# Unread matmuls at batch starts, an earlier base for the last block, and the first expert requested alone

## The chip, the cores and the metric

One core of one Trainium2 chip runs the whole program. The metric is the device time of one execution in microseconds (us). A difference is judged against the spread of repeated executions of both kernels on the same chip.

## What is computed

`x` has 12,500 rows of 256, and 212,500 directed edges (with one self loop a row) are sorted by target. Cut to what matters:

```python
xn = _layernorm(x)
agg = segment_sum(xn[src], dst) / counts                       # mean over the neighbours
gnn = relu(agg @ W_l.T + b_l + xn @ W_r.T) + xn
q, k, v = elu(xn@wq+bq)+1, elu(xn@wk+bk)+1, xn@wv+bv            # 8 heads of 32
mix = ((q @ (k.T @ v)) / (q @ k.sum(0))) @ wo + bo             # linear attention
x1 = x + gnn + mix
y = _layernorm(x1)
logits = mean(y, rows) @ Wr + br                               # one routing decision for all rows
p = softmax(logits); p = softmax(p * scale); w, e = top_k(p, 2); w = softmax(w)
h = sum_i w_i * (gelu(y @ W1[e_i] + b1[e_i]) @ W2[e_i] + b2[e_i])
out = x1 + _layernorm(h + y) * gamma + beta
```

## The kernel before, in words

Stage 1 (up to about 142 us) normalises the rows, writes them to DRAM as a table of two f16 parts (`xn_table`), and turns the edge lists.

Stage 3 (142 to 2760 us) sums the neighbours. The rows are cut into 49 blocks of 256 targets. A block has 34 tiles of 128 edges (29 in the last block). For each tile POOL gathers 128 rows of the table into its slot of the ring (L672), DVE makes a one-hot matrix (L1504), and PE multiplies the two in two f16 matmuls (L1243, L1244, "the rows"), adding into one of two PSUM banks of `pa`. The tiles come in 8 batches a block, which begin at k = 0, 4, 8, 13, 17, 21, 25 and 30. POOL may be eight batches ahead: it gathers batch q of the next block once `batch_used` says that PE has used batch q of this one, and once `idx_ready` says that ACT has written its indices (L738). ACT takes a strip of 64 finished sums (L768) four times a block; strips begin at k=4, 13, 21 and 30. DVE joins the strips (L1513 to L1522) and ACT scales them (L775).

Between the rows PE does other work, at tiles written out by hand:
- blocks 0 to 9 ("shadow"): the keys of the attention (`key_work`, L982, L995, L1005);
- blocks 10 to 19 ("doubled"): the dense work of two blocks in each (`double_work`), with `normalizers` at k=12, 13 and k=29, 30;
- blocks 20 to 48 ("late", a loop from about 1295 us on): the dense work of one block (`dense`). At k=1, 2 stands `mixed_product` of the block before (L1094), at k=9 `turn_sums` (L1145, waits for L775), at k=12, 13 `neighbour_product` (L1094), at k=14 `turn_xn` (L1070, taken by ACT L781), at k=16, 17 `queries` (L1078), which ACT reads in L790 (exponent) and L793, at k=24, 25 `normalizers` (L1087, waits for DVE's L1548; DVE goes on with L1554, a reciprocal L1556 and L1558), at k=27 `turn_y` (L1134, taken by ACT L815), and at k=29, 31 `base` (L1105, L1094, L1108, L1109), after which ACT makes the next rows (L762) and SP asks for the x rows after them (L296).

ACT's queue in a late block is L768, L790, L793, L807, L738 for two batches, L768, L815, L738 for three batches, L768, L762, L738, L768, L775, L738, L768, L800, L781. Each instruction waits in its queue behind those before it.

Behind the last rows of the last block PE does both halves of `base`, then the rest of that block's dense work. A mean over all y gives the logits (L1258). DVE finds the two best experts in small steps (L1669 to L1702) and writes both indices with one copy (L1696, `picked`). SP waits for it, reads both registers (L613), and asks for W1, b1 and W2 of each expert (L615, L617, L620), and then b2 (L624). ACT and DVE split each W1 into two parts (L950, L1719).

Stage 5 (about 2813 us to the end) runs both experts on 512 rows at a time: L1275 (first layer), L1290 (second).

## Time and profile before

| | us |
|---|---|
| runs | 3372.62, 3365.61, 3381.5 |
| median | 3372.62 |
| the profiled execution, its time | 3382.15 |
| its span | 3380.7 |
| stage 1 | 0 to 142 |
| shadow blocks | 142 to 695 |
| doubled blocks | 695 to 1295 |
| late blocks | 1295 to 2760 |
| last block's rest, routing | 2760 to 2813 |
| experts | 2813 to 3380 |

A time in a row is counted in us from the start of the span. PE is TensorE's matrix product, DVE VectorE, ACT ScalarE, POOL GpSimd, SP the engine that issues most transfers. A row of an engine in time gives the start, the length, the line, the tiles written and read, how many instructions it stands for, and in brackets the idle time before it and what ended that. "remote" and "issue" are releases for which the profile has no name.
### The profile page before, as it was taken

What the parts mean: (1) busy time and instruction counts of PE and PEld (TensorE: products, weight loads), DVE (VectorE), ACT (ScalarE), POOL (GpSimd) and SP (SyncE); (2) the same over time, 40 slices, a digit from 0 to 9 for tenths busy, and PEclk for the clock granted to TensorE, in tenths of its full rate; (3) what the DMA queues carried; (4) which work ended last, traced back from release to release, by engine and by line L of the source; (5) the groups of instructions that cost most, each with busy time, mean ns of one, the idle gap of its engine ahead of it and who ended that gap; (6) DMA issues with size and microseconds to landing.
All of it is one profiled execution on the core that took longest, in us unless ns stands there. A gap on an engine that the chain in (4) does not pass through costs nothing.

```text
span 3380.7 us, 35327 instructions
## 1 busy us (share of the span) xinstructions
PE 2141.0 (63%) x10858; PEld 1625.9 (48%) x10858; DVE 1423.6 (42%) x3244; ACT 955.7 (28%) x2221; POOL 1607.6 (48%) x1679
## 2 busy tenths in 40 slices
PE   1147667657766775565465454654555557999998
PEld 0135445545444553343343333433333346999997
DVE  7612222334444443332333323333333335777777
ACT  4512222222222221111111111111111114656565
POOL 1256666665555555666566665666566640000000
PEclk9978788878777777767767777677777778999999
DMA  6633333333333333333333333333333322222221
GB/s 210 215 101 115 112 111 110 91 102 106 100 97 100 98 93 103 98 103 98 98 101 100 103 101 96 100 101 102 98 98 103 103 70 77 75 63 68 74 74 58
DMA packets 205191, 340.31 MB, mean 101 GB/s; under 512 B 33118, under 2 KB 151131, under 8 KB 205115
## 3 DMA queue, kind: packets, MB, share of 16 engines
q0 software_dynamic: 80160, 219.14, 22.6%
q1 hardware_dynamic: 124538, 119.81, 11.1%
q8 instruction: 42, 0.69, 0.1%
q10 hardware_dynamic: 416, 0.39, 0.1%
q14 instruction: 35, 0.28, 0.0%
HBM read 288.01 MB, written 51.20 MB: 100 GB/s over the span
## 4 chain that ended last, share of the span: by engine, by line
PE 41%; another core or an unknown queue 34%; issue 9%; ACT 7%; DVE 7%; DMA 1%; ACTq 1%; SPq 0%; DVEq 0%
PE pd L1290 8%; PE pd L1094 6%; PE pa L1275 4%; PE pc L1275 4%; PE pa L1244 3%; PE pd L995 2%; PE pa L1243 2%; PE pd L1105 2%; PE pd L1087 2%; PE pd L1134 1%; PE pc L1005 1%; PE pc L1145 1%; PE pd L1108 1%; PE pd L1109 1%
## 5 line engine op out<-in xcount | busy, mean ns | idle before, releaser
L672 POOL DMA_INDIRECT ring<-xn_table,idxb x1661 | 1598.8, 963 | 1150.4 <-issue 633.2
L1244 PE MATMUL pa<-ring,ohh 128*128 128x257 f16 x1661 | 472.0, 305 | 76.4 <-issue 76.2
L1243 PE MATMUL pa<-ring,ohh 128*128 128x256 f16 x1661 | 469.9, 304 | 75.0 <-issue 65.9
L1087 PE MATMUL pd<-work,KS_s 128*128 128x256 f32 x196 | 107.8, 652 | 472.3 <-DVE work L1548 395.5
L1290 PE MATMUL pd<-parts 128*128 128x256 f32 (+1 forms) x1568 | 312.2, 282 | 1.8 <-DVE parts L1747 1.8
L1087 PEld LDWEIGHTS pd<-work,KS_s 128*128 128x128 f32 x196 | 49.7, 313 | 489.0 <-DVE work L1548 404.6
L1244 PEld LDWEIGHTS pa<-ring,ohh 128*128 128x128 f16 x1661 | 179.8, 108 | 197.0 <-issue 121.8
L1094 PE MATMUL pd<-mats,work 128*128 128x256 f32 x784 | 260.1, 463 | 0.9 <-DVE work L1530 0.9
L1290 PEld LDWEIGHTS pd<-parts 128*128 128x128 f32 (+1 forms) x1568 | 253.1, 188 | 10.3 <-DVE parts L1747 2.4
L1504 DVE TENSOR_TENSOR ohh<-pc,edges 128x512 f16<-128x512 f32 (+1 forms) x307 | 214.2, 718 | 98.4 <-PE pa L1244 64.6
L768 ACT ACTIVATE ring<-pa 128x257 f32<-128x257 f32 x196 | 75.4, 385 | 620.1 <-remote 313.5
L1243 PEld LDWEIGHTS pa<-ring,ohh 128*128 128x128 f16 x1661 | 180.8, 109 | 129.3 <-issue 86.7
L1513 DVE TENSOR_TENSOR ring<-ring 64x514 f32<-64x514 f32 x49 | 33.5, 684 | 445.0 <-ACT ring L768 445.0
L1290 PE MATMUL pd<-W_lo_t,parts 128*128 128x256 f32 x784 | 219.7, 280 | 0.0
L1094 PEld LDWEIGHTS pd<-mats,work 128*128 128x128 f32 x784 | 164.2, 232 | 114.2 <-issue 91.7
L1548 DVE SCALAR_TENSOR_TENSOR work<-work 128x512 f32<-128x512 f32 x49 | 33.9, 692 | 425.3 <-ACT work L793 413.7
L790 ACT ACTIVATE work<-pd,bq_c 128x256 f32<-128x256 f32 x98 | 41.1, 471 | 535.0 <-remote 523.4
L995 PE MATMUL pd<-mats,yT 128*128 128x256 f32 x392 | 124.2, 472 | 103.0 <-ACT yT L723 102.5
L1145 PE MATMUL pc<-ident,ring 128*128 128x128 f32 x160 | 39.9, 397 | 209.1 <-ACT ring L775 209.1
L1556 DVE RECIPROCAL work<-work 128x512 f32<-128x512 f32 x49 | 164.3, 3353 | 1.7
L995 PEld LDWEIGHTS pd<-mats,yT 128*128 128x128 f32 x392 | 90.2, 242 | 128.9 <-ACT yT L723 112.8
L1290 PEld LDWEIGHTS pd<-W_lo_t,parts 128*128 128x128 f32 x784 | 147.2, 188 | 9.1
(205 smaller groups left out, 3726.1 us busy)
## 6 DMA issues: line engine op xcount, KB each, us to landing
ring<-xn_table,idxb POOLq DMA_INDIRECT x1661
yT<-in_x SPq DMA_DIRECT2D x48, 512.0 KB
xn_table<-ring SPq DMA_DIRECT2D x24, 512.0 KB, 5.4
x_rows<-work SPq DMA_DIRECT2D x48, 256.0 KB
y_rows<-work SPq DMA_DIRECT2D x48, 256.0 KB
work<-y_rows SPq DMA_DIRECT2D x24, 512.0 KB, 4.3
work<-x_rows SPq DMA_DIRECT2D x24, 512.0 KB, 3.7
out<-work SPq DMA_DIRECT2D x24, 512.0 KB, 3.1
```

The lines of the kernel that those rows point to most:

```text
L672: pool.indirect_dma_start(out=msgs[:, k, 0:PARTS * D], out_offset=None, in_=xn_table[:, :], in_offset=bass.IndirectOffsetOnAxis(ap=idxb[:, ...
L768: nc.scalar.activation(strips[:, (NS * u + t + 1) % KEPT, 0:D + 1], pa[:, t % 2, 0:D + 1], ACT.Copy)\
L995: ins = mm(pd[0:n, 2 + pr, (t % 2) * D:(t % 2 + 1) * D], xTb[kq % 2][:, c, t * P:t * P + n], wk_s[:, c, :], start=c == 0, stop=c == C - 1)
L1087: ins = mm(pd[:, 0, c * BN:(c + 1) * BN], KS_s[:, c, :], pq[:, c * BN:(c + 1) * BN], start=True, stop=True)
L1094: ins = mm(pd[:, 2 + h, at:at + D], a[:, c * BN + h * P:c * BN + (h + 1) * P], w[:, c, :], start=False, stop=last and c == C - 1, skip_gro ...
L1145: ins = nc.tensor.transpose(to[:, c * BN + g * P:c * BN + (g + 1) * P], strips[:, NS * u + 2 * g + 1, c * P:(c + 1) * P], ident[:, :])
L1243: mm(pa[:, t % 2, 0:D], oh[:, slot, :], msgs[:, k, 0:D], start=begins, stop=False, skip_group_check=True)
L1244: ins = mm(pa[:, t % 2, 0:D + 1], oh[:, slot, :], msgs[:, k, D:2 * D + 1], start=False, stop=ends, skip_group_check=True)
L1275: ins = mm(hbank(f)[:, 0:w], wp[:, e, c, fc * P:(fc + 1) * P], yp[u][:, c, 0:w], start=c == 0 and wp is W1_hi and yp is y_hi, stop=c == C ...
L1290: ins = mm(pd[0:n, 2 * u + t // 2, (t % 2) * D:(t % 2 + 1) * D], hp[:, t * P:t * P + n], wp[:, f, :], start=f == 0 and t % 2 == 0 and hp i ...
L1504: V.tensor_tensor(oh[:, slot:slot + m, :], bc(row[:, c0:c0 + WIN], m), where, ALU.is_equal)\
L1556: V.reciprocal(qb, qb).then_inc(s["nrm_rec"], 1)
```

## The change

Three edits.

(a) `occupy(b, q, bank)` issues a number of unread matmuls at the first tile of each batch, ahead of that tile's dense work and ahead of its waits for one-hots and gathers. Each is an f32 matmul of the identity against 252 columns of `blo_b` into columns 260 to 511 of the bank of `pa` that the tile uses; the sums use columns 0 to 256, and nobody reads the others. Late blocks get `FILL`, doubled blocks `FILL_DOUBLE`, shadow blocks one of two `FILL_KEYS`. The wait for `strip_taken` moves ahead of the fills and the dense work.

(b) In the last block both normalizers and the first half of `base` are issued at k=21 and the second half at k=25, in place of the normalizers at k=24 and 25 and of both halves behind the last rows.

(c) DVE writes the first expert's index as soon as it is known and raises `picked`; SP then reads that register alone and asks for this expert's W1 in two halves, b1 and W2, and only then waits for the second. ACT and DVE split W1 in three pieces, and the first layer's first two column groups wait for the first piece only.

```diff
+        W1_PIECES = [(0, "w1_loaded0", 16, slice(0, F // 2)), (0, "w1_half1", 32, slice(F // 2, F)),
+                     (1, "w1_loaded1", 32, slice(0, F))]
...
-            sp.wait_ge(s["picked"], 1)
-            chosen = [sp.value_load(pick[0:1, n:n + 1], min_val=0, max_val=NE - 1) for n in range(2)]
-            for n, e in enumerate(chosen):
-                sp.dma_start(W1_s[:, n, :, :], W1[bass.ds(e, 1), :, :].rearrange("a (c p) f -> p (a c) f", p=P))\
-                    .then_inc(s[f"w1_loaded{n}"], 16)
+            chosen = []
+            for n in range(2):
+                sp.wait_ge(s["picked"], n + 1)
+                e = sp.value_load(pick[0:1, n:n + 1], min_val=0, max_val=NE - 1)
+                chosen.append(e)
+                if n == 0:
+                    sp.dma_start(W1_s[:, n, :, 0:F // 2], expert_rows(e, 0, F // 2)).then_inc(s["w1_loaded0"], 16)
+                    sp.dma_start(W1_s[:, n, :, F // 2:F], expert_rows(e, F // 2, F)).then_inc(s["w1_half1"], 16)
+                else:
+                    sp.dma_start(W1_s[:, n, :, :], expert_rows(e, 0, F)).then_inc(s["w1_loaded1"], 16)
...
-            for e in range(2):
-                act.wait_ge(s[f"w1_loaded{e}"], 32)
-                nc.scalar.activation(W1_hi[:, e, :, :], W1_s[:, e, :, :], ACT.Copy).then_inc(s["w1_hi_made"], 1)
+            for e, loaded, count, fs in W1_PIECES:
+                act.wait_ge(s[loaded], count)
+                nc.scalar.activation(W1_hi[:, e, :, fs], W1_s[:, e, :, fs], ACT.Copy).then_inc(s["w1_hi_made"], 1)
...
+            FILL_KEYS = ((0, 3, 0, 0, 0, 0, 0, 1), (4, 3, 0, 1, 4, 3, 0, 5))
+            FILL_DOUBLE = (0, 0, 0, 6, 0, 0, 0, 3)
+            FILL = (0, 3, 7, 1, 0, 7, 5, 0)
+            UNREAD = slice(D + 4, 512)
+
+            def occupy(b, q, bank):
+
+                if isinstance(b, int) and b < 2 * DELAY:
+                    n = (FILL_KEYS[b % 2] if b < DELAY else FILL_DOUBLE)[q]
+                else:
+                    n = FILL[q]
+                for _ in range(n):
+                    mm(pa[:, bank, UNREAD], ident[:, :], blo_b[:, 0:512 - (D + 4)], start=False, stop=False,
+                       skip_group_check=True)
...
+            LAST_BASE = (21, 25)
...
-                if k in DENSE:
+                if is_int(b, NB - 1) and k in LAST_BASE:
+                    if k == LAST_BASE[0]:
+                        for c in range(C):
+                            normalizers(b, c)
+                    base(b, LAST_BASE.index(k), u)
+                elif k in DENSE and not (is_int(b, NB - 1) and k > LAST_BASE[0]):
...
                     for k in ks:
+                        slot = k % SLOTS
+                        t = LO[k] // STRIP
+                        begins = is_int(b, 0) and k == 0 or k > 0 and LO[k] != LO[k - 1]
+                        ends = last_block and k == LAST - 1 or k + 1 < TB and LO[k] != LO[k + 1]
+                        if begins:
+                            wait(pe, s["strip_taken"], NS * b + t)
+                        if k == ks[0]:
+                            occupy(b, q, t % 2)
                         if isinstance(b, int) and b < DELAY:
                             key_work(b, k, u)
...
-                if last_block:
-                    for h in range(2):
-                        base(b, h, u)
...
-                    pe.wait_ge(s["w1_split"], e + 1)
+                    pe.wait_ge(s["w1_split"], 1 if f < FC // 2 else e + 2)
...
             first_at(row(R_W), row(R_M, 1), 0)
+            V.tensor_copy(pick[:, 0:1], row(R_I, 1)).then_inc(s["picked"], 1)
...
-            V.tensor_copy(pick[:, :], row(R_I, 2)).then_inc(s["picked"], 1)
+            V.tensor_copy(pick[:, 1:2], row(R_I, 1, 1)).then_inc(s["picked"], 1)
...
-            split_w1(0)
+            split_w1(0)
+            split_w1(1)
```

## Rows read from the trace of the kernel before

**Rows 1.** The page: busy time, share of the span and instructions; shares of the last chain.

```profile
PE 2141.0 (63%) x10858; PEld 1625.9 (48%) x10858; DVE 1423.6 (42%) x3244; ACT 955.7 (28%) x2221; POOL 1607.6 (48%) x1679
...
PE 41%; another core or an unknown queue 34%; issue 9%; ACT 7%; DVE 7%; DMA 1%; ACTq 1%; SPq 0%; DVEq 0%
```

**Rows 2.** By stretch, core 0: length, busy (instructions) of each engine, TensorE clock, DMA.

```profile
1300.00:2650.00 1350.00, 726.29 (x3323) 500.02 (x3323) 443.41 (x931) 225.71 (x723) 837.47 (x876) 0.73 0.34 100
...
2813.00:3380.00 567.00, 555.12 (x3552) 502.56 (x3552) 399.90 (x902) 329.15 (x524) 0.00 (x0) 0.99 0.22 70
...
1795.94:1848.54 52.60, 27.13 (x130) 18.50 (x128) 17.15 (x36) 8.77 (x28) 32.59 (x35) 0.76 0.34 100
803.30:861.80 58.50, 39.54 (x186) 27.84 (x184) 26.17 (x58) 15.22 (x45) 32.36 (x34) 0.85 0.35 104
```

**Rows 3.** POOL in time, late block: start, us, instruction [idle before <-releaser].

```profile
1795.94 0.94 POOL L672 DMA_INDIRECT ring<-xn_table,idxb  x1 [6.34 <-ACT idxb L738]
...
1820.81 1.33 POOL L672 DMA_INDIRECT ring<-xn_table,idxb  x1 [3.91 <-issue]
...
1848.54 0.95 POOL L672 DMA_INDIRECT ring<-xn_table,idxb  x1 [6.35 <-ACT idxb L738]
```

**Rows 4.** The page's costliest groups: busy, mean ns, idle before, its releaser.

```profile
L672 POOL DMA_INDIRECT ring<-xn_table,idxb x1661 | 1598.8, 963 | 1150.4 <-issue 633.2
...
L790 ACT ACTIVATE work<-pd,bq_c 128x256 f32<-128x256 f32 x98 | 41.1, 471 | 535.0 <-remote 523.4
```

**Rows 5.** ACT in time, the same late block.

```profile
1792.42 0.84 ACT L790 ACTIVATE work<-pd,bq_c 128x256 f32<-128x256 f32 x2 [14.67 <-remote]
...
1799.88 0.39 ACT L738 ACTIVATE idxb<-edges 128x4 int32 x3
...
1818.04 1.09 ACT L762 ACTIVATE work<-work,nmr_a,rstd_a 128x256 f32<-128x256 f32 x2 [13.19 <-remote]
```

**Rows 6.** PE in time, the same late block.

```profile
1778.99 1.03 PE L1078 MATMUL pd<-work,mats 128*128 128x256 f32 x4
...
1794.77 1.22 PE L1087 MATMUL pd<-work,KS_s 128*128 128x256 f32 x2 [13.18 <-DVE work L1548]
...
1801.69 0.59 PE L1108 MATMUL pd<-ring,ident 128*128 128x256 f32 x2
1802.12 0.59 PE L1109 MATMUL pd<-work,ident 128*128 128x256 f32 x2
...
1823.58 1.11 PE L1145 MATMUL pc<-ident,ring 128*128 128x128 f32 x4 [3.98 <-ACT ring L775]
```

**Rows 7.** PE and ACT in time, another late block.

```profile
2260.55 1.91 PE L1078 MATMUL pd<-work,mats 128*128 128x256 f32 x4
...
2264.78 0.84 ACT L790 ACTIVATE work<-pd,bq_c 128x256 f32<-128x256 f32 x2 [6.58 <-remote]
```

**Rows 8.** By stretch of 2 us, the late block of rows 3.

```profile
1796.00:1798.00 2.00, 2.00 (x9) 1.43 (x8) 0.69 (x1) 0.00 (x0) 1.69 (x2) 0.50 0.51 162
1800.00:1802.00 2.00, 2.00 (x8) 1.15 (x7) 1.97 (x2) 0.27 (x3) 1.58 (x2) 1.00 0.45 131
1822.00:1824.00 2.00, 0.42 (x2) 0.42 (x3) 1.13 (x4) 1.00 (x3) 1.39 (x3) 0.50 0.22 66
```

**Rows 9.** PE in time, a doubled block at the lower clock.

```profile
827.21 1.06 PE L1108 MATMUL pd<-work,ident 128*128 128x256 f32 x2
```

**Rows 10.** POOL in time, a doubled block.

```profile
853.32 0.94 POOL L672 DMA_INDIRECT ring<-xn_table,idxb  x1 [4.26 <-PE pa L1244]
```

**Rows 11.** PE in time, the end of stage 3 and the routing.

```profile
2779.27 1.12 PE L1105 MATMUL pd<-blo_b,ones 1*128 1x512 f32 x2
...
2785.13 1.89 PE L1094 MATMUL pd<-M_s,work 128*128 128x256 f32 x8
...
2812.96 1.19 PE L1275 MATMUL pa<-parts 128*128 128x512 f32 x2 [6.90 <-DVE W_lo_t L1719]
```

**Rows 12.** SP's queue in time: the first request of an expert's weights.

```profile
2806.03 0.41 SPq L615 DMA_DIRECT2D mats<-in_L_ffn_W  x1
```

More of the change, by code:

```diff
@@ L252, in build_layer @@
         names = """waits_taken iota_set iota_float iota_placed mask_step wk_loaded consts_set ident_set raw_padded raw_loaded raw_float raw_turned raw_taken
-            flag_sum flag_added flag_set w_loaded biases_loaded wlr_turned wlr_taken bias1_set
+            flag_sum flag_added flag_set w_loaded biases_loaded wlr_turned wlr_taken
             x_loaded0 x_loaded1 x_loaded2 x_loaded3 p1_bn p1_mv p1_rstd p1_stats rows_unscaled hi_made lo_made xn_ready xn_stored0 xn_stored1 xn_stored2 xn_stored3 xt_turned xt_made
@@ L261, in build_layer @@
             route_step route_exp logits_made ysum_made mean_made picked gates_made gates_spread gates_taken
-            w1_loaded0 w1_loaded1 w2_loaded0 w2_loaded1 b2_loaded w1_hi_made w1_split w2_hi_made w2_split yh_made yl_made hh_made hl_made
+            w1_loaded0 w1_half1 w1_loaded1 w2_loaded0 w2_loaded1 b2_loaded w1_hi_made w1_split w2_hi_made w2_split yh_made yl_made hh_made hl_made
             l2_done b2_made yin_loaded0 yin_loaded1 yb_made xb_made
@@ L609, in _, with expert_rows @@
             over_blocks(sp, transfers)
-            sp.wait_ge(s["picked"], 1)
-            chosen = [sp.value_load(pick[0:1, n:n + 1], min_val=0, max_val=NE - 1) for n in range(2)]
-            for n, e in enumerate(chosen):
-                sp.dma_start(W1_s[:, n, :, :], W1[bass.ds(e, 1), :, :].rearrange("a (c p) f -> p (a c) f", p=P))\
-                    .then_inc(s[f"w1_loaded{n}"], 16)
+            def expert_rows(e, f0, f1):
+                return W1[bass.ds(e, 1), :, f0:f1].rearrange("a (c p) f -> p (a c) f", p=P)
+            chosen = []
[8 more added lines that the diff above has]
+                    sp.dma_start(W1_s[:, n, :, :], expert_rows(e, 0, F)).then_inc(s["w1_loaded1"], 16)
                 sp.dma_start(b1_c[:, n, :], b1[bass.ds(e, 1), :].rearrange("a (c p) -> p (a c)", p=P),
                              allow_slow_non_contiguous=True)\
-                    .then_inc(s[f"w1_loaded{n}"], 16)
+                    .then_inc(s["w1_half1" if n == 0 else "w1_loaded1"], 16)
                 sp.dma_start(W2_s[:, n * FC:(n + 1) * FC, :],
@@ L1234, in stage3 @@
                             pe.wait_ge(s[f"gathered{q}"], batch_gathers(b, q))
-                        slot = k % SLOTS
-                        t = LO[k] // STRIP
-                        begins = is_int(b, 0) and k == 0 or k > 0 and LO[k] != LO[k - 1]
-                        ends = last_block and k == LAST - 1 or k + 1 < TB and LO[k] != LO[k + 1]
-                        if begins:
-                            wait(pe, s["strip_taken"], NS * b + t)
                         if is_int(b, 0) and k == 0:
@@ L1465, in _ @@
             dve.wait_ge(s["wk_loaded"], 32)
-            V.tensor_scalar(b1k_b[:, :], b1k_b[:, :], 1.0, None, ALU.add).then_inc(s["bias1_set"], 1)
-            dve.wait_ge(s["bias1_set"], 1)
+            V.tensor_scalar(b1k_b[:, :], b1k_b[:, :], 1.0, None, ALU.add).then_inc(s["mask_step"], 1)
+            dve.wait_ge(s["mask_step"], 4)
             dve.wait_ge(s["p1_stats"], len(TABLE_GROUPS))
@@ L1714, in _, with split_w1 @@
             split_y(0, 0)
-            def split_w1(e):
-                dve.wait_ge(s["w1_hi_made"], e + 1)
-                V.tensor_tensor(W1_lo[:, e, :, :], W1_s[:, e, :, :], W1_hi[:, e, :, :], ALU.subtract)\
+            def split_w1(piece):
+                e, _, _, fs = W1_PIECES[piece]
+                dve.wait_ge(s["w1_hi_made"], piece + 1)
+                V.tensor_tensor(W1_lo[:, e, :, fs], W1_s[:, e, :, fs], W1_hi[:, e, :, fs], ALU.subtract)\
                     .then_inc(s["w1_split"], 1)
@@ L1735, in mix_b2 @@
                 V.tensor_scalar(b2a, b2_b[:, 0, :], gate_b[:, 0:1], None, ALU.mult).then_inc(s["mask_step"], 1)
-                dve.wait_ge(s["mask_step"], 4)
+                dve.wait_ge(s["mask_step"], 5)
                 V.scalar_tensor_tensor(out=b2m, in0=b2_b[:, 1, :], scalar=gate_b[:, 1:2], in1=b2a, op0=ALU.mult,
@@ L1803, in stage5 @@
                     if is_int(q, 0) and f < 3:
-                        (lambda: split_w1(1), lambda: split_w2(1), mix_b2)[f]()
+                        (lambda: split_w1(2), lambda: split_w2(1), mix_b2)[f]()
                     if f == 0 and later:
```

## The prediction

> **What bounds the kernel now.** I read the busy shares first, then the chain that ended last, then the costliest groups. No engine is full: TensorE is busy 63% of the span and POOL 48%, and the chain gives 41% to PE and 34% to releases that the profile can't name [rows 1]. So the answer differs by stage, and the table by stretch shows it [rows 2]. From 2813 us on (the two experts) PE is busy 555 of 567 us at a clock of 0.99: full, and no wait there to fill. From 1300 to 2650 us PE is busy 726 of 1350 us at a mean clock of 0.73, and POOL 837. There POOL's gathers set the pace: a run of 17 lasts from 1795.94 to 1820.81 - 3.91 = 1816.90, one every 1.25 us, so the 34 of a block need 42.5 us, and a block takes 52.6 (1795.94 to 1848.54) [rows 3]. The ten missing microseconds are two gaps a block: 6.34 us ahead of batch 3, waiting for ACT's indices L738, and 3.91 us ahead of batch 7. Gaps of that kind are all that a change in this stage can return: L672's idle time is 1150.4 us [rows 4]; less 1,660 usual pauses of 0.30 us it is 650, the wait for the table at the start still in it. That is the outer bound.
>
> What ends those gaps? ACT's exponent L790 stands idle 523.4 us for a release "remote" [rows 4]. In the block shown it starts at 1792.42, and by PE's records the queries L1078 that it reads had begun their second half at 1778.99 [rows 5, 6]. It starts 2.8 us after the last gather of the run has ended (1795.94 - 6.34 = 1789.60). L762 starts at 1818.04 although L1109 was recorded by 1806, 1.1 us after that run ended. So while POOL gathers, late PE results reach the others only when the run is over: the two gaps are partly a closed loop, run, release, indices, next run. One block speaks for the loop's stiffness: L1078's second half is recorded at 2260.55 there, hardly two microseconds before the end of its run, L790 starts at 2264.78 [rows 7], and the gap behind it is of the usual size. PE's queries may come 10 us late, or early, and the period is the same.
>
> The Trainium skill ("Perfetto Trace Analysis", "Tensor Engine Instruction (MATMUL, LD_WEIGHTS)") says that a matmul's recorded end is estimated, and that its semaphore goes out only after PSUM has acknowledged the writes. By that PE's gap in front of L1087 need not be free time, and fills put there could queue behind unfinished work; the trace neither shows nor excludes it.
>
> **The clock.** PE stalls 13.18 us ahead of L1087 and 3.98 us ahead of L1145 [rows 6]. In both the granted clock falls to its lower level (0.50, 1.2 GHz) and is still there when PE resumes: 0.50 in 1822 to 1824 and in 1796 to 1798, 1.00 in 1800 to 1802 [rows 8]. So some 5 us of work behind L1087 (1794.77 to the 1800 of that row) and, by the same table cut finer, 3 us behind L1145 run at half speed: 2.5 and 1.5 us that a full clock would give back.
>
> **Part (a), the unread matmuls.** A fill is one f32 matmul of the identity against 252 columns. Its nearest rows are L1108 and L1109, the identity against 256 columns: two records each, starting 0.43 us apart at the full clock [rows 6]. At half each record is 1.06 us long in place of 0.59 [rows 9], and I take 0.85 us a fill. Late blocks get 0+3+7+1+0+7+5+0 = 23, so 9.9 us at the full, 19.6 us at the half clock, and the 29 of them 287 to 567 us of PE time. Doubled blocks get 9 (90 in all), shadow blocks 4 or 20 (120): another 90 to 180 us. None of it costs anything where PE waits anyway, and PE is idle 25.5 us a late block (52.6 less 27.1 [rows 2]).
> - k=4 (3) and k=8 (7) stand ahead of L1145, which waits for the chain of strip, join and scaling. PE has 4 us there [rows 6]; ten fills take 4.3 us warm, 8.5 us cold. So they overhang by 0 to 4.5 us, and give back the 1.5 us of a cold resumption.
> - k=21 (7) stand ahead of L1087's 13 us stall: 3 us, hidden. But they run at its beginning, so 10 us of idle time stay behind them and PE resumes cold as before: the 2.5 us there are not won.
> - k=25 (5) stand between the two halves of L1087, right after the resumption, at the half clock: 4.3 us (2.1 warm) that nothing hides. Behind them wait L1554, the reciprocal, L1134, L815 and ACT's L738 x3 at 1799.88, the indices of batches 5, 6 and 0 [rows 5]. POOL needs the first of them for the ninth gather of its run, 1795.94 + 8 x 1.25 = 1805.9. L738 would come at 1802 to 1804.2: in time, with 1.7 us to spare in the worse case.
> - k=13 (1): 0.4 us.
> The strip_taken wait moved ahead of the fills holds back only neighbour_product's second half at k=13, behind a strip taken 5 us before: nothing.
>
> What reaches POOL? Behind L1145 up to 1.5 us a block, if the earlier queries shorten the gap ahead of batch 3; nothing, if the loop holds. I take 0.9 us, nearer to the upper end than a mean of the two, because some releases do come through in the first eight microseconds of a run: 28 x 0.9 = **-25 us** (bounds: -42 from the clock, +126 from 4.5 us of overhang).
>
> In the doubled blocks PE is busy 39.5 of 58.5 us at a mean clock of 0.85 [rows 2], and POOL waits for PE's rows (4.26 us at 853.32 [rows 10]). A mean of 0.85 between two levels, 0.5 and 1, means 30% of the time at half. But the nine fills (3.8 us warm, 7.7 cold) stand at k=13 (6) and k=30 (3), each time between the halves of a normalizer, right behind its stall. They warm the clock by delaying L1134 and the rows behind. The row that POOL waits for (k=12) is ahead of them, and the five gathers that it then starts (6.3 us) cover 5.1 us of fills. Gain and loss nearly cancel: **-5** (bounds -4.26 x 10 = -43, that wait gone in each block, to +7.7 x 10 = +77). Shadow blocks: PE mostly waits for rows and keys; 12 fills a block on the mean; **-5** (-50 to +50).
>
> The Trainium skill ("TensorE: Matmul & The Clock Gate", "Loop structure matters more than you think") has a loop that waits for a transfer between its matmuls drop to the slow clock, as here. It asks for dense real work, not for filler; by its reading alone, all 4 us a block would come back, and the sum would be 3382 - 112 before the rest.
>
> **Part (b), the last block.** Both normalizers and base(0) move to k=21, base(1) to k=25. They are the same instructions. Before, base ran behind the last rows from 2779.27 to 2785.13, and L1145, which waits for the last strip's join, came 1.7 us later, behind eight L1094 [rows 11]. Moved ahead, the 5.9 us are off that place; but the last rows then end up to 5.9 us plus five fills later, and join and scaling (5 us from the strip to L1145) start behind them. PE waits for little in this stretch, so I expect little: **+1** (-3 to +6).
>
> **Part (c), the first expert.** The first index is copied before the second is searched, some eight DVE steps of about 0.18 us, 1.5 us, earlier; SP reads one register instead of two, and the first W1 request, at 2806.03 [rows 12], carries half. The two steps that split it, ACT's and DVE's, halve too: L1275, at 2812.96 after 6.90 us of waiting [rows 11], could start 2.5 us sooner. The second half and its queue come at the old time or 0.5 us later. **-2.5** (-4 to +1).
>
> **Sum.** -25 - 5 - 5 + 1 - 2.5 = -36.5. The profiled execution has a span of 3380.7 and a time of 3382.15 us, 9.5 above the median of the runs. 3382.15 - 36.5 = 3345.7; less 9.5: **3336 us**, 1.1% faster. Chance 0.36.
>
> **Rivals.**
> 1. The loop holds and hides everything: fills in idle time, earlier queries released at the run's end as before. For it: the block of [rows 7], and the two gaps ahead of batch 3, 6.34 and 6.35 us [rows 3]. Left are the tail and a few us in the doubled blocks: 3365 us. Chance 0.26. That the fills don't warm the clock at all belongs here.
> 2. Slower: the fills push a release out of the part of a run in which it still comes through. The place is k=8 and k=25: if L1145, through L1070 and L781, or L1134 passes that point, the indices of batch 5 come only after POOL has stopped once more, and each stop costs what the gap ahead of batch 7 costs, 3.91 us [rows 3]. In 28 blocks that is +109: 3482 us; in a third of them, or by the overhang alone (1 to 2 us a block), 3400 to 3430. It decides when L738 x3 comes more than 6 us later than now, or L1145 more than 3. Chance 0.30.
> 3. The queries get ahead of the point: batch 3's indices are there before batch 2 is gathered, and the 6.34 us go in every late block. 28 x 6.34 = 178, so 3195 us. PE would have to be 3 us earlier and has 1.5. Chance 0.08.
>
> **How the numbers follow.** About 0.5% (17 us) is what a measurement of this kernel can tell from no change. Faster holds the forecast (0.36) and rival 3 (0.08): 0.44. Same 0.26. Slower 0.30. The range leaves out rival 3 and the full case of rival 2, some 0.15 to 0.2 together: 3240 to 3465. As cases of both signs are likely, the forecast's own range is 3280 to 3356.
>
> **What would show it.** POOL's period of 52.6 us in the late loop is the first thing to read: 51.7 if I am right, 52.6 for rival 1, 56 for rival 2, 46 for rival 3. The clock should be 1.00 when L1145 resumes and 0.50 when L1087 does. L738 x3 should come 2 to 4 us later against the run's start, and the run of 17 gathers stay whole. In the tail, L1275 should start earlier against L1258, and L1145 about as late behind the last gather. I am wrong if the clock at L1145's resumption is still 0.50, or if the runs of gathers have other lengths than 17.

## The result and the profile after

| | us |
|---|---|
| before, median of 4 runs | 3373.14 (3365.61 to 3381.5) |
| changed, median of 4 runs | 3440.96 (3430.06 to 3470.29) |
| ratio, with its 95% interval | 1.0227 (1.0193 to 1.0262) |
| changed, profiled execution | 3451.18, span 3449.7 |

The change costs 2.3%. Lines of `kernel.py` have moved: L672 is now L683, L738 L749, L781 L792, L790 L801, L1070 L1081, L1078 L1089, L1087 L1098, L1134 L1145, L1145 L1156, L1244 L1278, L1275 L1306, L768 L779, L775 L786, L1094 L1105, L1105 L1116, L1504 L1535, L1513 L1544, L1516 L1547, L1548 L1579, L1558 L1589, L1719 L1752; the fills are L1172.

The changed kernel's page, the parts of [rows 1] and [rows 4]:

```profile
PE 2442.2 (71%) x12612; PEld 1916.6 (56%) x12612; DVE 1424.2 (41%) x3246; ACT 952.4 (28%) x2222; POOL 1605.7 (47%) x1679
...
PE 42%; another core or an unknown queue 29%; issue 14%; DVE 7%; ACT 6%; DMA 1%; ACTq 0%; SPq 0%; POOL 0%; DVEq 0%; POOLq 0%
...
L683 POOL DMA_INDIRECT ring<-xn_table,idxb x1661 | 1596.9, 961 | 1217.3 <-issue 548.8
L1172 PE MATMUL pa<-blo_b,ident 128*128 128x252 f32 x1754 | 475.9, 416 | 35.0 <-issue 33.5
```

PE is busy 301 us more than before: the 877 fills take 475.9 us, and the other work, at a higher clock, some 175 us less. In the chain the share of unnamed releases falls from 34% to 29% and that of "issue" rises from 9% to 14%. Yet POOL's idle time grows by 67 us, from 1150.4 to 1217.3, and the span by 69: nearly the whole loss is gathers that start later. By stretch, and by two pieces of one late block, with the columns of [rows 2]:

```profile
1300.00:2650.00 1350.00, 896.03 (x4250) 661.05 (x4250) 421.17 (x887) 212.95 (x691) 793.77 (x830) 0.82 0.32 95
...
2297.89:2355.18 57.29, 35.72 (x174) 26.98 (x173) 17.33 (x36) 8.58 (x28) 32.58 (x35) 0.79 0.31 92
2320.00:2322.00 2.00, 2.00 (x11) 1.80 (x10) 0.00 (x0) 0.00 (x0) 1.68 (x2) 1.00 0.43 127
2347.00:2349.00 2.00, 1.59 (x4) 1.32 (x5) 0.00 (x0) 0.36 (x1) 0.00 (x0) 0.50 0.00 0
```

The clock did rise: 0.82 in the late loop against 0.73. The gain that it was to bring isn't there. One late block takes 57.29 us, of which 15.0 us are its two gaps (11.95 and 3.02) and 42.3 its gathers with their usual pauses. POOL in time, as in [rows 3]:

```profile
2297.89 0.94 POOL L683 DMA_INDIRECT ring<-xn_table,idxb  x1 [12.08 <-ACT idxb L749]
...
2315.60 0.95 POOL L683 DMA_INDIRECT ring<-xn_table,idxb  x1 [3.02 <-remote]
...
2355.18 0.94 POOL L683 DMA_INDIRECT ring<-xn_table,idxb  x1 [11.95 <-ACT idxb L749]
```

The gaps are now ahead of batch 3 (11.95 or 12.08 us, before 6.34) and ahead of batch 6 (3.02 us at 2315.60, before none), and the one ahead of batch 7 is gone. Runs are of 12 and 22 gathers instead of 17 and 17. Not every late block is like this one: of the runs that start in blocks 20 to 47, 23 are of 12 gathers, 9 of 22, 20 still of 17 and 19 of other, mostly shorter, lengths (before, 52 of 58 are of 17). Summed over these blocks, the gaps ahead of batch 6 grow by 47 us and those ahead of batch 7 shrink by 59, so the new stop replaces the old one and by itself adds nothing. The gaps ahead of batch 3 grow by 67 us (from 177 to 244), those ahead of batches 1 and 2 by 20. PE and ACT in the same block, as in [rows 6] and [rows 5]:

```profile
2295.45 3.14 PE L1172 MATMUL pa<-blo_b,ident 128*128 128x252 f32 x14
...
2299.10 0.59 PE L1098 MATMUL pd<-work,KS_s 128*128 128x256 f32 x2
...
2299.75 2.29 PE L1172 MATMUL pa<-blo_b,ident 128*128 128x252 f32 x10
2301.87 0.59 PE L1098 MATMUL pd<-work,KS_s 128*128 128x256 f32 x2
...
2319.50 3.14 PE L1172 MATMUL pa<-blo_b,ident 128*128 128x252 f32 x14
...
2322.70 0.60 PE L1156 MATMUL pc<-ident,ring 128*128 128x128 f32 x4
...
2326.88 0.60 PE L1081 MATMUL pd<-ident,work 128*128 128x128 f32 x4
...
2347.41 2.07 PE L1089 MATMUL pd<-work,mats 128*128 128x256 f32 x4 [19.49 <-ACT work L792]
```

```profile
2304.25 0.39 ACT L749 ACTIVATE idxb<-edges 128x4 int32 x3
...
2318.65 0.91 ACT L786 ACTIVATE ring<-ring,cnts 128x256 f32<-128x256 f32 x2 [1.95 <-DVE cnts L1553]
...
2346.76 0.60 ACT L792 ACTIVATE work<-pd 128x512 f32<-128x512 f32 x1 [12.71 <-remote]
2351.66 0.84 ACT L801 ACTIVATE work<-pd,bq_c 128x256 f32<-128x256 f32 x2 [4.30 <-PE pd L1089]
```

Read the last two PE rows with the last two ACT rows. PE turned the rows (L1081) at 2326.88; ACT copied them (L792) only at 2346.76, 3.5 us behind the end of a run of gathers (2355.18 - 11.95 = 2343.23). PE waited 19.5 us for that copy, did the queries at the lower clock (0.50 in 2347 to 2349), and L801 came at 2351.66. The same steps in the kernel before, POOL, PE and ACT, in the run that ends ahead of the first gather of [rows 3]:

```profile
1768.22 1.32 POOL L672 DMA_INDIRECT ring<-xn_table,idxb  x1 [3.77 <-issue]
...
1776.52 0.60 PE L1070 MATMUL pd<-ident,work 128*128 128x128 f32 x4
...
1777.15 0.60 ACT L781 ACTIVATE work<-pd 128x512 f32<-128x512 f32 x1
```

There the copy L781 starts as soon as the rows are turned, 8.3 us into the run, and only L790 is withheld. In the change one more step of the chain stands behind the end of the run: L792, queries and L801 take 4.9 us plus 0.84, and the gap has grown by 5.6.

This holds beyond the one block. In the traces of the nine kernels that met this condition (the two here, and e1 to e4 and e16 to e18 below) I took blocks 21 to 47, 243 blocks in all. In 47 of them the copy starts behind the last gather of the run, and the gap ahead of batch 3 is 8.6 to 12.2 us. In the other 196 it starts earlier, and the gap is never over 7.8 us. The kernel before has no block of the first kind, the change 17 of 27. The rows are turned 8.1 us into their run of gathers in the kernel before and 9.8 us in the change (medians).

By the starts of the gathers the loss splits so (us, changed against before): blocks 0 to 19, 1090.6 against 1097.2; blocks 20 to 47, 1546.7 against 1478.1; block 48, 43.8 against 40.7; from the last gather's start to the end, 626.5 against 622.5. The others nearly cancel (-6.6 + 3.1 + 4.0 = +0.5); the late blocks hold 68.6 of 69.1 us.

### The profile page after: what moved, and what is told of

It reads as the page before. It is cut to its first block, busy times and chain, and to the rows that moved or that the text cites. A ratio compares the mean times of both kernels' runs of the same rounds, so it can differ in the third digit from the quotient of the medians.

```text
span 3449.7 us, 38842 instructions
## 1 busy us (share of the span) xinstructions
PE 2442.2 (71%) x12612; PEld 1916.6 (56%) x12612; DVE 1424.2 (41%) x3246; ACT 952.4 (28%) x2222; POOL 1605.7 (47%) x1679
## 4 chain that ended last, share of the span: by engine, by line
PE 42%; another core or an unknown queue 29%; issue 14%; DVE 7%; ACT 6%; DMA 1%; ACTq 0%; SPq 0%; POOL 0%; DVEq 0%; POOLq 0%
PE pd L1321 8%; PE pa L1172 5%; PE pd L1105 4%; PE pc L1306 4%; PE pa L1306 4%; PE pc L1016 3%; PE pd L1089 3%; PE pd L1006 2%; PE pa L1278 2%; PE pa L1277 2%; PE pd L1116 2%; PE pd L1098 1%; DVE bst L1369 1%; ACT ring L779 1%
## 5 line engine op out<-in xcount | busy, mean ns | idle before, releaser
L683 POOL DMA_INDIRECT ring<-xn_table,idxb x1661 | 1596.9, 961 | 1217.3 <-issue 548.8
L1172 PE MATMUL pa<-blo_b,ident 128*128 128x252 f32 x1754 | 475.9, 416 | 35.0 <-issue 33.5
L1277 PE MATMUL pa<-ring,ohh 128*128 128x256 f16 x1661 | 440.2, 287 | 49.7 <-issue 39.5
L1278 PE MATMUL pa<-ring,ohh 128*128 128x257 f16 x1661 | 441.2, 288 | 37.1 <-issue 36.5
L1172 PEld LDWEIGHTS pa<-blo_b,ident 128*128 128x128 f32 x1754 | 358.3, 215 | 98.8 <-issue 51.8
L1089 PE MATMUL pd<-work,mats 128*128 128x256 f32 x392 | 147.8, 515 | 344.5 <-ACT work L792 285.1
L1089 PEld LDWEIGHTS pd<-work,mats 128*128 128x128 f32 x392 | 91.8, 259 | 371.6 <-ACT work L792 296.5
L779 ACT ACTIVATE ring<-pa 128x257 f32<-128x257 f32 x196 | 74.8, 382 | 785.8 <-remote 537.9
L1535 DVE TENSOR_TENSOR ohh<-pc,edges 128x512 f16<-128x512 f32 (+1 forms) x307 | 214.8, 718 | 186.1 <-remote 138.0
L1278 PEld LDWEIGHTS pa<-ring,ohh 128*128 128x128 f16 x1661 | 170.0, 102 | 163.8 <-issue 83.6
L1105 PE MATMUL pd<-mats,work 128*128 128x256 f32 x784 | 225.6, 412 | 42.7 <-DVE work L1561 28.5
L1105 PEld LDWEIGHTS pd<-mats,work 128*128 128x128 f32 x784 | 142.9, 199 | 141.5 <-issue 92.5
L1016 PE MATMUL pc<-yT 128*128 128x257 f32 x392 | 125.2, 475 | 84.5 <-DVE yT L1417 47.6
L1579 DVE SCALAR_TENSOR_TENSOR work<-work 128x512 f32<-128x512 f32 x49 | 34.0, 693 | 329.7 <-ACT work L804 254.7
L1098 PE MATMUL pd<-work,KS_s 128*128 128x256 f32 x196 | 71.6, 452 | 137.8 <-DVE work L1579 111.4
L1568 DVE TENSOR_TENSOR work<-work,pd 128x512 f32<-128x512 f32 x49 | 33.7, 687 | 316.7 <-ACT work L811 175.1
```

Source lines behind the costliest of these rows:

```text
L683: pool.indirect_dma_start(out=msgs[:, k, 0:PARTS * D], out_offset=None, in_=xn_table[:, :], in_offset=bass.IndirectOffsetOnAxis(ap=idxb[:, ...
L779: nc.scalar.activation(strips[:, (NS * u + t + 1) % KEPT, 0:D + 1], pa[:, t % 2, 0:D + 1], ACT.Copy)\
L1016: ins = mm(pc[:, c, 0:KXW], phi[0:n, t, c * P:(c + 1) * P], xnb[kq % 2][0:n, t, :], start=kq == 0 and t == 0, stop=kq == NQ and t == len(T ...
L1089: ins = mm(pd[:, 1, o * BN:(o + 1) * BN], wq_s[:, c, o * P:(o + 1) * P], xT2[:, c * BN:(c + 1) * BN], start=c == 0, stop=c == C - 1)
L1105: ins = mm(pd[:, 2 + h, at:at + D], a[:, c * BN + h * P:c * BN + (h + 1) * P], w[:, c, :], start=False, stop=last and c == C - 1, skip_gro ...
L1172: mm(pa[:, bank, UNREAD], ident[:, :], blo_b[:, 0:512 - (D + 4)], start=False, stop=False, skip_group_check=True)
```

## Experiments

**Two conditions.** All runs of one group were on one chip, beside runs of the kernel before. In two of the five groups of experiments, and in the result above, the median of the kernel before is 3373 to 3389 us; in the three others it is 2863 to 2864, with nothing changed. The chip numbered 1 was met in both conditions. I call them withholding and free, by what their traces show (e9_before_again). Ratios are always against the kernel before in the same group. A kernel that was run again in the other condition has a second or third label.

**e1_no_fills, e2_late_fills, e3_early_fills, e4_k8_fills** (withholding). In `occupy`'s tables:

```diff
 e1: FILL_KEYS, FILL_DOUBLE and FILL all zero
 e2: FILL_KEYS and FILL_DOUBLE zero, FILL as in the change
 e3: FILL zero, the others as in the change
 e4: as e2, with FILL = (0, 0, 7, 0, 0, 0, 0, 0)
```

> The changed kernel with every fill count at zero: the last block's base ahead of its last rows, the first expert asked for alone, and the earlier strip wait stay. Theory A (the loss is a chain in the late blocks: the fills put L1145 and the turning of the rows later in a run of gathers, so that the copy L792 is withheld to the run's end and the queries start only then): 3365 to 3375 us, gap ahead of batch 3 back at 6.3 us, period 52.5, the end of the program within 4 us of before. Rival B (the loss is in the last block or the routing): still above 3400.

> Fills only in the late blocks, 23 a block; none in the shadow and doubled blocks. Theory A: about 3440 us, gaps ahead of batch 3 of 10 to 12 us in most late blocks. If instead the fills of the first twenty blocks shift the late loop into its bad pattern: about 3375.

> Fills only in the shadow and doubled blocks, none in the late blocks. Theory A: 3360 to 3370 us, block 20 begins some 7 us earlier than in the kernel before, and the late period is 52.5 us. Rival (the early fills start a bad pattern): 3400 or more.

> Of all fills only the seven at k=8 of the late blocks, ahead of L1145. Theory A with k=8 as the place: 3420 to 3445 us, L792 withheld to the end of a run. If the fills at k=25 or the sum of several places do it: 3365 to 3385.

Measured: e1 1.0042 (1.0009 to 1.0076), e2 1.0062 (1.0029 to 1.0096), e3 1.0086 (1.0065 to 1.0107), e4 1.0054 (1.0021 to 1.0087). So there is a loss with no fills at all, of 0.4%, which I can't place: e1's profiled run is the fastest of its seven, most of its late blocks take 52.9 us (the kernel before had 52.5 on its chip), and its tail is 0.7 us longer than before. The fills at k=8 alone add 0.1% to that, less than these intervals can tell from nothing, so they are not the place by themselves, and my Theory A fell in that form. e2 has exactly the late fills of the change and lost much less here, 0.2% more than e1, which the intervals don't tell from nothing either (10 us in its blocks 20 to 47 against those of e1, 3 against those of e4), with periods that jump between 50.3 and 57.7 us. The early fills alone, e3, lost more than the late ones. One profile of such a pattern says little; several are needed.

The first twenty blocks show the same. e1, e2 and e4 have identical code in them, and by their profiles block 20 begins 1088.8, 1074.6 and 1097.1 us after the first gather. A difference of 22 us there is within what one code does. So what the early fills do in this condition is open: 1122.1 in e3, 1070.7 in the later e17.

**e5_after_again, e6_late_without_k25, e7_k25_fills, e8_k25_short_f16** (free). The trace of the change showed where the pattern turns: five fills at k=25, 2.1 us (2299.75 to 2301.87), put the last row of batch 6 some 9 us into its run in place of 6.7, and POOL then stopped ahead of batch 6.

```diff
 e6: FILL_KEYS and FILL_DOUBLE zero, FILL = (0, 3, 7, 1, 0, 7, 0, 0)
 e7: the same, with FILL = (0, 0, 0, 0, 0, 0, 5, 0)
 e8: the same, with FILL = (0, 0, 0, 0, 0, 0, 10, 0), and in occupy
-                    mm(pa[:, bank, UNREAD], ident[:, :], blo_b[:, 0:512 - (D + 4)], start=False, stop=False,
+                    mm(pa[:, bank, D + 4:D + 4 + P], ones_h[:, :], ones_h[:, :], start=False, stop=False,
```

> The changed kernel as it is, once more, beside the others on one chip. What it tells: how much of its 2.3% is there on another chip and in another execution. Theory C (the k=25 fills delay the signal that batch 6 is used, POOL's runs become 12 and 22 instead of 17 and 17, and the turning of the rows then falls into the withheld part of the long run): runs of 12 and 22 in most late blocks, gaps ahead of batch 3 of 10 to 12 us, and 1.5 to 2.5% over before. If the earlier loss was an accident of one execution: under 1%.

> No fills in the first twenty blocks; late fills as in the change, but none at k=25 (18 a block). Theory C: runs of 17 and 17, L1098 recorded about 1.3 us into its run, period 52.5 to 53, time as of the kernel without fills (0 to +0.5% over before). If the places k=4, 8 and 21 do the harm: split runs and +0.6% or more as with all late fills.

> Of all fills only the five at k=25 of the late blocks, at the lower clock 4.3 us ahead of the rows of batch 6. Theory C: the signal that batch 6 is used comes 9 us or more into the run instead of 7, a gap appears ahead of batch 6 (k=25), runs of 12 and 22, and +1 to +2%. If the place is not the cause: no gap ahead of batch 6, 0 to +0.5%.

> As many PE instructions at k=25 as in the kernel before it in this list (ten), but each a 128-column f16 product, some 0.06 to 0.11 us, about 1 us together. If what counts is how late PE comes in time: no split, as without fills. If what counts is how many instructions PE has finished in the run: the same split and loss as with five f32 fills.

Measured, and unforeseen: before 2863.03 us. e5, the change itself, 0.9962 (0.9949 to 0.9975); e6 0.9931 (0.9908 to 0.9953); e7 0.9961 (0.9946 to 0.9975); e8 0.9965 (0.9954 to 0.9977). Theory C could not be tested: nothing is withheld here. For the same reason e8 tells nothing of time against number of instructions.

**e9_before_again, e10_after_third, e11_without_k25_again, e12_k25_again** (free): the kernel before, the change, e6 and e7 once more.

> The kernel before, as it is, for its profile on this chip. The two chips seen so far differ: on one kind its time is 3373 to 3389 us and POOL's gathers come in runs with gaps of 3.8 and 6.3 us, on the other it is 2863 us. On the first kind: runs of 17, queries' signal withheld some 12 us, block period 52.5 to 53. On the second: no gap over 0.6 us between gathers, PE results reach ACT within 0.2 us, last gather about 1130 us after block 20 begins; time 1.00 of before.

> The changed kernel beside the kernel before on one chip. Theory C (delays withheld by the runs of gathers decide): where gathers withhold PE's results, 1.5 to 2.5% over before, runs of 12 and 22. Where they don't: 0.996 of before as in the run before, since POOL's gathers are the bound and the fills lie beside them.

> No early fills; late fills without the five at k=25. Theory C: where gathers withhold results, runs of 17 and 17, period 52.5 to 53, 0 to +0.5% over before; if the places k=4, 8 and 21 do the harm, split runs and +0.6% or more. Where they don't: 0.993 as before.

> Of all fills only the five at k=25. Theory C: where gathers withhold results, a gap ahead of batch 6, runs of 12 and 22, +1 to +2% over before; if the place is not the cause, 0 to +0.5% and runs of 17. Where they don't: 0.996.

Measured: e9 0.9998 (0.9988 to 1.0008), e10 0.9987 (0.9977 to 0.9996), e11 0.9947 (0.9930 to 0.9963), e12 0.9970 (0.9957 to 0.9982). The kernel before in the free condition: its page (chain by line, the gathers' group), POOL's waits, and ACT in a late block:

```profile
POOL 37%; PE 37%; issue 13%; DVE 5%; ACT 3%; DMA 3%; POOLq 1%; SPq 0%; ACTq 0%; DVEq 0%
...
L672 POOL DMA_INDIRECT ring<-xn_table,idxb x1661 | 1604.4, 966 | 637.2 <-issue 494.7
```

```profile
POOL ring L672 <- issue: 494.7, 1624, 0.3
POOL ring L672 <- DMA xn_table<-ring: 131.6, 1, 131.6
POOL ring L672 <- PE pa L1244: 8.8, 29, 0.3
```

```profile
1638.26 0.84 ACT L790 ACTIVATE work<-pd,bq_c 128x256 f32<-128x256 f32 x2 [2.31 <-PE pd L1078]
```

A gather takes what it takes in the other condition (966 ns, there 963), but POOL now waits for nothing after the first gather: the longest wait is 0.3 us, the chain runs over L672, and L790 starts when its queries are done, with a named releaser ("PE pd L1078") in place of "remote". Of the 516 us between the two spans, 513 are POOL's idle time (1150.4 against 637.2).

Where the gathers are the bound, only the tail and the gathers' own length can change. Tail, PE in time, first the kernel before, then e11, then e10:

```profile
2256.85 2.07 PE L1105 MATMUL pd<-blo_b,ones 1*128 1x512 f32 x2
...
2270.96 0.60 PE L1145 MATMUL pc<-ident,ring 128*128 128x128 f32 x4
```

```profile
2246.08 1.12 PE L1116 MATMUL pd<-blo_b,ones 1*128 1x512 f32 x2
...
2253.74 0.65 PE L1156 MATMUL pc<-ident,ring 128*128 128x128 f32 x4 [1.56 <-ACT ring L786]
```

```profile
2260.33 2.29 PE L1172 MATMUL pa<-blo_b,ident 128*128 128x252 f32 x10
...
2270.20 0.66 PE L1156 MATMUL pc<-ident,ring 128*128 128x128 f32 x4 [1.56 <-ACT ring L786]
```

The last gathers start at 2250.64, 2244.56 and 2255.74. So the scaled sums are turned 20.3 us behind it before, 9.2 in e11, 14.5 in e10. Before, `base` runs behind the last rows and on the lower clock (5.7 us a half, 2256.85 to the next half at 2262.57); moved ahead of them it is hidden. The five k=25 fills, in sight at 2260.33, stand between its halves. By themselves they cost nothing there: e12, of the same group, has L1156 9.3 us behind the last gather. Only with the other fills of that block is it 14.5 us (e10) and 12.1 (e5).

**e13_k25_third, e14_without_k25_third, e15_no_fills_again** (free): e7, e6 and e1 again.

> Of all fills only the five at k=25 of the late blocks. Theory C, where gathers withhold results: a gap ahead of batch 6, runs of 12 and 22, +1 to +2% over before. If the place is not the cause: runs of 17, 0 to +0.5%. Where gathers run without a gap: 0.996 to 0.997 as twice before.

> Late fills at k=4, 8, 13 and 21, none at k=25, none in the first twenty blocks. Theory C, where gathers withhold results: runs of 17 and 17, period as without fills, 0 to +0.5% over before. If these places do the harm: split runs, +0.6% or more. Where gathers run without a gap: 0.993 to 0.995 as twice before.

> No fills at all; the last block's base ahead of its last rows and the first expert alone stay. Where gathers withhold results: 0 to +0.4% over before as in its first run. Where gathers run without a gap: the last block's L1156 some 9 us behind the last gather in place of 20, so 10 to 12 us less than before, 0.996; if the fills without k=25 were worth something of their own there, this kernel is 5 us slower than e14.

Measured: e13 0.9964 (0.9950 to 0.9978), e14 0.9933 (0.9916 to 0.9950), e15 0.9962 (0.9948 to 0.9976). Without any fill the gain of parts (b) and (c) is there, 12 us. The late fills without k=25 add 7 us to it (2844.77 against 2852.12), and the k=25 fills alone add nothing (2851.37). Together with the others the k=25 fills take the 7 us away again: the change has 2853.69 us (e5) where e6 has 2844.48, and 2861.13 (e10) where e11 has 2848.80. It also has the early fills, but its first twenty blocks are within 2.3 us of theirs.

Those 7 us are in the gathers. Their usual length is 0.95 us, but some take 1.1 to 1.6. Counted over the whole trace there are 97 such in e15 (31 us over 0.95 in sum), 96 in e9 (32 us), 80 in e14 (24 us) and 63 in e11 (19 us); in blocks 20 to 47 alone 44 in e15 (14 us), 27 in e14 (7 us) and 19 in e11 (5 us). POOL and DVE in time, e15:

```profile
1362.21 0.94 POOL L683 DMA_INDIRECT ring<-xn_table,idxb  x1 [0.30 <-issue]
1363.45 1.29 POOL L683 DMA_INDIRECT ring<-xn_table,idxb  x1 [0.30 <-issue]
1365.05 0.95 POOL L683 DMA_INDIRECT ring<-xn_table,idxb  x1 [0.30 <-issue]
```

```profile
1363.24 0.69 DVE L1544 TENSOR_TENSOR ring<-ring 64x514 f32<-64x514 f32 x1 [6.23 <-ACT ring L779]
1363.96 0.76 DVE L1547 TENSOR_TENSOR ring<-ring 64x257 f32<-64x257 f32 x2
```

The gather that starts inside L1544 takes 1.29 us. L1544 and L1547 read both inputs from SBUF. In e15, 21 of the 27 gathers that overlap just these two are long (15 of 29 in e11). Other DVE instructions with two SBUF inputs do the same: of the gathers that overlap a one-hot L1535 and L1589, 23 of 38 are long, of those with a one-hot and L1579 14 of 43, and of those with only a one-hot that takes its row from `iota_f` in SBUF, 17 of 48. The same L1535 with its row in PSUM (`pc`, from about block 10 on) makes none of 137 long, and with DVE idle it is 0 of 719 (0 of 747 in e11). All 97 long gathers of e15, and all 63 of e11, overlap a DVE instruction that reads two inputs from SBUF. The Trainium skill ("SBUF — State Buffer", "Who interferes with whom") has DVE and GpSimd share a port pair, over which a DVE instruction with two SBUF inputs contends with a GpSimd instruction that reads SBUF. These counts agree, if a gather counts as one that reads SBUF. Fills shift what DVE does against the gathers, and so how often they meet. That this is the way the 7 us come about is worked out from the counts, not tried by itself.

**e16_late_fills_again, e17_early_fills_again, e18_without_k25_fourth** (withholding again): e2, e3 and e6.

> All late fills, none in the first twenty blocks. Where gathers run without gaps: if the k=25 fills take the gain away, 0.996 to 0.998, and in the tail L1156 some 14 us behind the last gather in place of 9; if the early ones did, 0.993 to 0.995. Where gathers withhold results (Theory C): split runs and +0.5 to +2%.

> Fills in the first twenty blocks only. Where gathers run without gaps: 0.996 as without fills if they lie in cover, 0.998 or more if they cost something. Where gathers withhold results: +0.5 to +1% with the loss in blocks 0 to 19, as in its first run.

> Late fills without k=25, no early ones. Where gathers run without gaps: 0.993 to 0.995, and fewer gathers over 1.1 us (62 to 77 in place of 93 to 96). Where gathers withhold results (Theory C): runs of 17 and 17, 0 to +0.5%.

Measured: e16 1.0224 (1.0172 to 1.0277), e17 1.0061 (1.0040 to 1.0083), e18 1.0133 (1.0087 to 1.0179). On this chip the late fills alone make a loss as large as that of the change, and the early ones 0.6%. Taking the k=25 fills away takes 0.9% of 2.2% away, with intervals that just overlap. On the chip of e1 to e4 the same code behaved otherwise: late fills alone 0.6%, early ones 0.9%, none 0.4%. A kernel without fills was not run on this chip, so how much of these losses belongs to parts (b) and (c) is not known here. POOL in e18, a late block:

```profile
2207.81 0.95 POOL L683 DMA_INDIRECT ring<-xn_table,idxb  x1 [5.86 <-ACT idxb L749]
...
2232.57 1.32 POOL L683 DMA_INDIRECT ring<-xn_table,idxb  x1 [3.77 <-issue]
...
2260.46 0.95 POOL L683 DMA_INDIRECT ring<-xn_table,idxb  x1 [6.54 <-ACT idxb L749]
```

The run between the two gaps is 17 again, as Theory C wanted: over blocks 20 to 47 the gaps ahead of batch 6, less the usual pauses, add up to 4 us in e18, against 51 in the change, 35 in e16, 44 in e2, and 4 in the kernel before. But the rest of the loss stays, so the theory holds for the split and not for the whole. What all of it has in common is the wait for the copy of the turned rows (PE's waits: total, times, longest), in the kernel before, e17, e4, e18, e16 and the change:

```profile
PE pd L1078 <- ACT work L781: 13.9, 23, 8.7
```

```profile
PE pd L1089 <- ACT work L792: 19.7, 22, 12.5
```

```profile
PE pd L1089 <- ACT work L792: 49.2, 25, 16.6
```

```profile
PE pd L1089 <- ACT work L792: 83.9, 28, 14.5
```

```profile
PE pd L1089 <- ACT work L792: 164.8, 34, 19.4
```

```profile
PE pd L1089 <- ACT work L792: 285.1, 40, 20.7
```

From the start of block 20 to that of block 48 these take 1478.1, 1477.7, 1498.7 (e4, on the chip where e1 without fills takes 1492.2), 1501.0, 1522.2 and 1546.7 us. The other three traces of this condition fall in between: e1 24.3 us of this wait and 1492.2 us for the blocks, e3 31.6 and 1488.7, e2 133.3 and 1502.1. Over all nine, more of this wait goes with longer blocks, with two swaps of neighbours. These are single profiled executions, and those of e16, e17 and e18 are the fastest of their kernels (e17: 3358.19 us against a median of 3396.58), so the blocks of e17 look better here than the kernel is.

What is shown: the time is lost where the copy L792 starts only behind the end of a run (the 47 blocks against 196 above), and the k=25 fills split the runs (e16 against e18). That the late fills make the loss is shown on one chip (e16 against e17) and not on the other (e2 against e1). Not shown is which of k=4, 8 and 21 puts it there in e18, since k=8 alone hardly does.

## Why the prediction was wrong

The sign was wrong. The range, 3240 to 3465, held the time. Rival 2 had the direction and the path, "if L1145, through L1070 and L781, ... passes that point", but not the price: it expected one more stop ahead of batch 5 at 3.91 us, where the runs have a longer gap ahead of batch 3. Its 3482, or 3400 to 3430, with the measured 3441 in between, is in part luck. Step by step:

- **The bound and the loop** (runs of gathers withhold late PE results): right. The gaps are where the loss came.
- **The clock at L1145's resumption**: right, 1.00 (2320 to 2322). At L1087's it is full too (a pair of L1098 takes 0.59 us, where before it took 1.06 to 1.22), where 0.50 was expected; the cold resumption is now that of the queries.
- **The late blocks' term, -25 us**: this is the step that failed. The forecast put 0.9 us a block on that clock, with the argument that some releases come through in the first eight microseconds, and took POOL's run of 17 as unhurt. The same argument, read the other way, was the danger: a release that comes through can be lost. Measured is +2.45 us a block (68.6 / 28) in place of -0.9. It weighed 1.5 us of clock against "0 to 4.5 us of overhang" and took the gain, though the rival named 3 us as the point at which it turns. In the block shown the wait for L786 is over at 2319.56 and L1156 starts at 2322.70, behind the seven fills: an overhang of 3.1 us. In its place stands the copy L792, which starts behind the end of the run in 17 of 27 blocks (before, in none) and there puts some 5 us on the gap ahead of batch 3.
- **The distance to the run's start** has a second part that the forecast left out. L1156 lies 7.1 us behind its run's start at 2315.60, before it was 2.8 (1823.58 against 1820.81); but most of that is because the run starts five gathers earlier, ahead of batch 6. Against the first gather of batch 7 L1156 is 0.4 us late in this block. Over blocks 21 to 47 the median of that distance is 2.8 us before and 3.9 in the change, 4.9 in e18 and 5.2 in e16.
- **k=8**: 7 fills took 3.0 us (2319.50 to 2322.48, where rows follow), as priced. They alone are not enough (e4).
- **k=21**: priced as hidden at the beginning of L1087's stall. Wrong: PE's long stall moved forward to the queries, and the seven fills ran at 2295.45, 2.4 us ahead of the start of the next run. Their 3.0 us stand ahead of everything that PE has to do in it.
- **k=25**: 2.1 us as priced, and L738 x3 2.4 us later against its run (6.4 in place of 3.9), in time as I said. What I didn't look at is the other signal that passes there, the use of batch 6. It was late, and split the run. That stop, 3.0 us, took the place of the one ahead of batch 7; what it costs, as far as the traces show, is that the next run starts sooner and the rows turned in it lie deeper in it.
- **Doubled and shadow blocks**: forecast -10, the profile says -6.6, and identical code scatters by 22. Neither right nor wrong.
- **Part (b)**: forecast +1 (-3 to +6). e1 without fills has L1156 31.7 us behind the last gather (2794.79 against 2763.12), before 28.7: +3.0, within the bounds. With fills, which the forecast meant, it is 35.5: +6.8, just outside. In the free condition part (b) is worth -11 us, which the trace of before could not show, since there the last rows came late.
- **Part (c)**: forecast -2.5. From the turning of the sums to the first product of the experts, rows of e1 and of the change:

```profile
2794.79 0.66 PE L1156 MATMUL pc<-ident,ring 128*128 128x128 f32 x4 [1.56 <-ACT ring L786]
...
2817.40 1.19 PE L1306 MATMUL pa<-parts 128*128 128x512 f32 x2 [3.28 <-DVE W_lo_t L1752]
```

```profile
2858.71 0.66 PE L1156 MATMUL pc<-ident,ring 128*128 128x128 f32 x4 [1.56 <-ACT ring L786]
...
2881.31 1.19 PE L1306 MATMUL pa<-parts 128*128 128x512 f32 x2 [3.29 <-DVE W_lo_t L1752]
```

22.6 us in both, against 26.1 before [rows 11]; in the change 0.7 of it is given back later, in e1 1.2: -2.8 and -2.3. In other runs the same stretch takes up to 24.4 us (e18). Right within its bounds.

The rival of nothing changed leaned on [rows 7], a block whose queries came 10 us late without any loss. More of that block, in PE, ACT and POOL:

```profile
2248.53 0.60 PE L1070 MATMUL pd<-ident,work 128*128 128x128 f32 x4
...
2257.60 0.60 ACT L781 ACTIVATE work<-pd 128x512 f32<-128x512 f32 x1 [6.38 <-remote]
...
2268.30 0.94 POOL L672 DMA_INDIRECT ring<-xn_table,idxb  x1 [6.62 <-ACT idxb L738]
```

There the copy itself was withheld, by some 9 us, and let through at 2257.60, 4.1 us before the end of its run (2268.30 - 6.62 = 2261.68). The reading was true, and the trace of before already had the case: a late copy costs nothing as long as it and the queries still fall inside the run, and what was left out is how near to the end of the run it was.

## What to carry to other kernels

Where a stage has slack in time but its signals get through only in part of each period, ask of each signal on the way, not of the busy time, how far it is from the point at which it is held back; filler in front of it can cost a whole step of the chain (here some 5 us in a block). A clock that rises, here from 0.73 to 0.82, is worth nothing if the work that it speeds up ends in the same wait. Filler would belong behind the last signal that others need; no run here tried that. A change should be timed in each condition that the kernel is met in: this one is 2.3% slower in one and 0.1 to 0.4% faster in the other. Moving `base` and the first expert without any fill is 0.4% slower in one and 0.4% faster in the other; with the late fills but without k=25 it is 1.3% slower and 0.5 to 0.7% faster. No version tried beats the kernel before in both.

## What the runs showed of the hardware

- The same program takes 3373 to 3389 us or 2863 us (medians). In one condition signals of TensorE's results reach ACT and POOL up to 20 us after its records (L1081 at 2326.88, L792 at 2346.76) while POOL issues indirect gathers, and come through inside the run (L781 at 2257.60, 4.1 us before its end) or within 3.5 us of its last gather; in the other condition the longest wait of the queries for the copy is 0.2 us. Whether the products or only their signals are late, the profile doesn't tell. A gather takes 0.96 to 0.97 us in both, so it isn't the gathers' rate. What sets the condition is open.
- In that condition the turned rows came through at once 8.3 us into a run of gathers in one block of the kernel before, and those turned 11.3 us into one (2326.88 against 2315.60) in the change did not. It is no sharp limit: the block with 7.8 us above was withheld too.
- A gather that overlaps a DVE instruction with two SBUF inputs can take 1.1 to 1.6 us in place of 0.95 (21 of 27 of those beside the joins in e15, 15 of 29 in e11); with an idle DVE, or a one-hot whose row is in PSUM, never (0 of 719 and 0 of 137 in e15).
- An unread f32 matmul of 252 columns takes 0.43 us at the full clock (3.0 us for seven). The clock rises though nobody reads the results: the mean over the whole execution is 0.971 in e5 (all fills) and 0.868 in e9 (none), both in the free condition.
